# The same work in another order at three places: the opening, the end of the experts' stage, and the start of the second attention stage

## The chip, the core and the metric

The kernel runs on one core of a Trainium2 chip. The metric is the device time of one execution in microseconds; three runs of the kernel before gave 1770.38, 1770.89 and 1771.04, median 1770.89. Times in the trace count from the span's start.

## The reference

Six blocks with residual additions: an attention with 4 key heads, a cross attention over windows, a mixture of experts, then an attention with relative positions, a second cross attention and a second mixture of experts. The change touches the projections of the two self attentions (x is 2 batches of 1024 tokens of 256; 16 heads of 16) and the additions of the first experts' outputs:

```
# first self attention
q = (xn @ w_q).reshape(b, n, N_HEADS, D_HEAD).transpose(0, 2, 1, 3)
k = (xn @ w_k).reshape(b, n, KV_HEADS, D_HEAD).transpose(0, 2, 1, 3)
v = (xn @ w_v).reshape(b, n, KV_HEADS, D_HEAD).transpose(0, 2, 1, 3)
q = q * rf
k = k * rf
# first experts, last line
final = jnp.einsum('ebcm,bsec->bsm', expert_out, combine_mask)
# second self attention
qkv = (x @ W_qkv + b_qkv).reshape(b, s, 3, H, hd)
score = jnp.einsum('bhqd,bhkd->bhqk', q, k) + jnp.einsum('bhqd,qkd->bhqk', q, pe_k)
attn = jax.nn.softmax(score, axis=-1)
ctx = jnp.einsum('bhqk,bhkd->bhqd', attn, v) + jnp.einsum('bhqk,qkd->bhqd', attn, pe_v)
```

## The kernel before, in words

**Programs.** Each stage writes one program for each engine (PE, ACT, DVE, POOL, and SP, which issues the DMAs), and each engine works its program off in the order written. Engines meet at semaphores; between stages there is a barrier. So the order of the code is the order of the work, and an instruction that waits holds all that stands behind it on its engine.

**Splitting.** Queries and keys are needed to float32's precision in bf16 matmuls. Each tile of 128 x 512 (a unit) is split into three bf16 parts: high (a conversion), residue (tile minus high), middle (conversion of the residue), low (residue minus middle). The three parts go to DRAM with one store a unit, and are loaded back later in the layout that the matmuls want, 96 rows of six pairs of parts.

**Opening** (`Opening.run`). x is loaded in four groups, normalized, turned on PE (`turn`), and twelve units of q and k are made: `product` on PE, `rotate` on DVE (L396, L399), `high` on ACT (L319), `residue` on DVE (L408), the middle conversion on POOL (L353), `low` on DVE (L417), the store on SP (L237). There are four buffers of parts, and a unit may use one when the store of four units before has landed. From the fifth unit on, PE makes two tiles of values (L278) behind each product. From the seventh unit on, SP issues four loads of the first stage's queries and keys (L675, L679) behind a store, after all stores of the first half have landed.

**End of the experts' stage** (`experts`). While the last expert's outputs are stored and gathered again (POOL, 16 indirect DMAs for batch 1), batch 0's projections for the second attention are made, in eight pairs of a product and a value (`pair`), twelve units: `Heads.high` and `middle` on ACT (L565, L571), `residue`, `values` and `low` on DVE (L580, L593, L587), `store` on SP (L600), six buffers of parts. Between them DVE adds the gathered outputs of batch 1 to x (`add`, L2188, two a tile), sums up for the norm (`summed`, L2196 to L2201) and scales (`shifted`); ACT then normalizes (L2111) and PE turns (`turn`, L2050). The stage ends when every store has landed.

**Start of the second attention** (`attention1`). SP first issues the first group's twelve loads (four heads; L944 queries, L948 keys). Batch 1's projections follow in the same manner (five buffers), with three jobs called `relative` between them: PE multiplies the queries with the relative embeddings (L1169), ACT copies the result, POOL builds a band of it (`band_of`, L1272 and L1275; a band may be built when the one before has landed), SP writes the band to DRAM in a skewed layout (`band_out`, L1057) and reads it back into `dev` (`bands_in`, L1049), which POOL has set to zero before (L1301). Then 256 tiles follow: PE's scores (`row`, L1138), DVE's sum and maximum (L1341), ACT's exponentials, and so on. The first row waits for the last residue and value of the projections.

## Time and profile before

| | us |
|---|---|
| median of three runs | 1770.89 |
| profiled execution | 1768.36 |
| its span | 1766.6 |
| PE busy | 1562.5 (88%) |
| DVE busy | 1018.2 (58%) |
| ACT busy | 880.8 (50%) |
| POOL busy | 563.4 (32%) |

Shares over the whole span say little here, since the stages have different limits: PE bounds the experts and the tail, DVE the second attention. The three stretches of the change are short, and are read from the instructions in order of time, engine by engine, with what ended each idle time.

### The profile page before, as it was taken

To read this page: it belongs to the slowest core of one execution; us is meant where nothing else is said; L and a number is where in the kernel's file an instruction comes from. 1 tells how busy PE (TensorE), PEld (TensorE's weight loads), DVE (VectorE), ACT (ScalarE), POOL (GpSimd) and SP (SyncE) were. 2 spreads that over 40 slices of the span, in tenths; PEclk is the share of its full clock that TensorE was granted. 3 is DMA by queue.
4 is the path that set the end of the run, shared out by engine and by line. 5 is a ranking of instruction groups with operands and counts; after the bars stand their busy time and mean duration, and the time that the engine had idled before them with its cause. 6 is when DMAs were issued, how large, how long until landed. Compare 5 with 4: busy or idle time off the path is not lost. (4 is left out here: it accounts for less than half of the span.)

```text
span 1766.6 us, 34238 instructions
## 1 busy us (share of the span) xinstructions
PE 1562.5 (88%) x12792; PEld 1071.8 (61%) x12792; DVE 1018.2 (58%) x2084; ACT 880.8 (50%) x1468; POOL 563.4 (32%) x817
## 2 busy tenths in 40 slices
PE   7689989878479999999976799999999999996988
PEld 4233333256368767776753477777777777775544
DVE  6677777345332111111264788888888888873556
ACT  4156566632331111111134688888888888773421
POOL 3411111122313000000252455556555655542111
PEclk9799999997679999999987799999999999998999
DMA  5811111030123133221237796887868778645101
GB/s 153 237 26 29 24 24 24 2 132 22 39 75 131 63 119 128 87 86 60 61 112 153 208 222 195 203 205 200 205 200 202 210 197 200 185 137 174 49 12 36
DMA packets 209797, 213.06 MB, mean 121 GB/s; under 512 B 19652, under 2 KB 187218, under 8 KB 209506
## 3 DMA queue, kind: packets, MB, share of 16 engines
q1 hardware_dynamic: 204769, 197.24, 41.5%
q0 software_dynamic: 4864, 13.64, 2.3%
q8 instruction: 103, 1.69, 0.4%
q14 instruction: 61, 0.49, 0.1%
HBM read 128.82 MB, written 81.81 MB: 119 GB/s over the span
## 5 line engine op out<-in xcount | busy, mean ns | idle before, releaser
L1341 DVE CUSTOM_DVE_ANT_0 prob<-ps,dev 128x1024 f32<-128x1024 f32 x256 | 311.5, 1218 | 0.2 <-PE ps L1138 0.2
L1234 ACT ACTIVATE prob<-prob,nmax 128x1024 f32<-128x1024 f32 x256 | 293.3, 1146 | 8.3 <-DVE nmax L1341 8.3
L1158 PE MATMUL ps<-cst,prob 128*128 128x128 f32 x2048 | 279.4, 278 | 0.2
L2030 PE MATMUL ps<-xeT,w 128*128 128x384 f32 (+2 forms) x896 | 256.0, 447 | 5.1 <-DVE hT L2228 4.4
L1158 PEld LDWEIGHTS ps<-cst,prob 128*128 128x128 f32 x2048 | 228.3, 141 | 42.3 <-issue 21.0
L1370 DVE COPY probT<-ps 128x512 f32<-128x512 f32 x256 | 176.4, 689 | 104.1 <-PE ps L1158 104.0
L849 ACT ACTIVATE pT<-ps 128x512 f32<-128x512 f32 (+3 forms) x384 | 166.3, 495 | 119.3 <-PE ps L805 116.8
L887 DVE TENSOR_REDUCE nmax<-ps 128x1 f32<-128x128 f32 (+7 forms) x256 | 184.2, 753 | 69.1 <-PE ps L784 67.9
L2030 PEld LDWEIGHTS ps<-xeT,w 128*128 128x128 f32 x896 | 176.9, 198 | 77.6 <-DVE hT L2228 4.8
L2096 ACT ACTIVATE xT_c<-ps 128x256 f32<-128x256 f32 (+2 forms) x98 | 46.6, 476 | 326.0 <-PE ps L2030 325.9
L1244 ACT ACTIVATE probT<-ps 128x512 f32<-128x512 f32 x256 | 151.3, 591 | 102.4 <-PE ps L1158 102.2
L2228 DVE TENSOR_TENSOR hT<-ps,xT_c 128x256 f32<-128x256 f32 (+2 forms) x98 | 52.7, 538 | 223.4 <-ACT xT_c L2096 223.4
L1138 PE MATMUL ps<-ks,qs 96*128 96x512 bf16 (+4 forms) x768 | 155.7, 312 | 8.7 <-DVE vz L593 6.7
L1199 PE MATMUL ps<-probT,vg 128*18 128x128 f32 (+1 forms) x4096 | 135.9, 273 | 0.0
L2040 PE MATMUL ps<-vz,hT 128*128 128x256 f32 x560 | 124.2, 381 | 8.3 <-DVE hT L2228 8.3
L782 PE MATMUL ps<-ks,qs 96*128 96x512 bf16 (+3 forms) x384 | 107.5, 343 | 25.9 <-DVE nmax L887 17.7
L805 PE MATMUL ps<-qs,ks 99*128 99x512 bf16 (+3 forms) x384 | 110.0, 336 | 14.3 <-ACT pT L849 7.6
L875 POOL TENSOR_SCALAR_AFFINE_SELECT pT<-pT 128x512 f32<-128x512 f32 x64 | 40.6, 635 | 250.5 <-ACT pT L849 250.5
L2040 PEld LDWEIGHTS ps<-vz,hT 128*128 128x128 f32 x560 | 105.2, 190 | 24.9 <-DVE hT L2228 11.1
L2150 POOL DMA_DIRECT2D ybuf<-ye x32 | 20.4, 642 | 307.4 <-DVE ye L2251 307.4
L1199 PEld LDWEIGHTS ps<-probT,vg 128*18 128x18 f32 (+1 forms) x4096 | 106.4, 98 | 17.1 <-issue 16.6
L1281 POOL TENSOR_TENSOR wm<-pre,cst 128x256 f32<-128x256 f32 x128 | 93.9, 734 | 47.7 <-DMA pre<-skew_p 44.9
(317 smaller groups left out, 2167.4 us busy)
## 6 DMA issues: line engine op xcount, KB each, us to landing
dev<-skew_u SPq DMA_DIRECT2D x128, 256.0 KB, 3.6
skew_p<-prob SPq DMA_DIRECT2D x128, 256.0 KB, 3.3
w<-in_L_ffn_w SPq DMA_DIRECT2D x20, 896.0 KB, 6.3
skew_u<-cst SPq DMA_DIRECT2D x64, 256.0 KB, 4.0
pre<-skew_p SPq DMA_DIRECT2D x128, 128.0 KB, 2.9
qs<-qd SPq DMA_DIRECT2D x96, 128.0 KB, 3.8
ks<-kd SPq DMA_DIRECT2D x48, 256.0 KB, 5.8
vz<-in_L_ffn_w SPq DMA_DIRECT2D x10, 896.0 KB, 5.7
```

Of the source, the lines that this page charges most:

```text
L805: nc.tensor.matmul(ps[:, bank, 0:w], ks[:, j, kb * P:(kb + 1) * P], qs[:, j, r, q0:q0 + w], start=True, stop=True).then_inc(s_key, 1)
L849: nc.scalar.activation(pT[:, c % 2, r, 0:w], ps[:, ring_bank(job), 0:w], ACT.Exp).then_inc(s_exp, 1)
L887: nc.vector.tensor_reduce(nmax[:, n % 2, r * KB + a:r * KB + a + 1], slot[:, 0:w], AX.X, ALU.max, negate=True).then_inc(s_max, 1)
L1138: last = nc.tensor.matmul(ps[:, 2 * (t % 2) + lo // 512, lo % 512:lo % 512 + hi - lo], qs[:, n % 2, r, a * P:(a + 1) * P], ks[:, n % 2, r, ...
L1158: last = nc.tensor.transpose(ps[:, ring_bank(job), kb * P:(kb + 1) * P], prob_tile(t, (4 * h + kb) * P, (4 * h + kb + 1) * P), k.c("ident"))
L1199: last = nc.tensor.matmul(ps[r * VW:r * VW + wide, 7, q % 4 * P:q % 4 * P + P], vg[:, n % 2, r, kb, int(kb == a), 0:wide], probT[:, (HQ * ...
L1234: nc.scalar.activation(prob_tile(t, 0, S), prob_tile(t, 0, S), ACT.Exp, bias=nmax[:, t % 4:t % 4 + 1], scale=-1.0).then_inc(s_exp, 1)
L1244: nc.scalar.activation(probT[:, t % SLOTS, 0:512], ps[:, ring_bank(job), :], ACT.Copy).then_inc(s_evA, 1)
L1341: nc.vector.tensor_tensor_reduce(out=prob_tile(t, 0, S), in0=scores, in1=dev_tile(t), scale=-1.0, scalar=3.0e38, op0=ALU.add, op1=ALU.min, ...
L1370: nc.vector.tensor_copy(probT[:, t % SLOTS, 512:S], ps[:, ring_bank(job), :]).then_inc(s_evD, 1)
L2030: last = nc.tensor.matmul(ps[:, a + z * wide + h, 0:cols], w[:, j, c, f * P:(f + 1) * P], xeT[:, c, h * cols:(h + 1) * cols], start=(c == ...
L2040: last = nc.tensor.matmul(ps[0:w, a + t // 2, t % 2 * D:(t % 2 + 1) * D], hT[:, f, o:o + w], w2[:, j, f, :], start=(f == 0), stop=(f == FC ...
```

## The change

- **Opening:** the sixteen value products come behind all products; ACT makes the middle conversions, POOL the low subtractions; ACT's first two high conversions come ahead of two copies of turned tiles.
- **Order of units in `Heads`:** the first eight heads' queries and keys of both half sequences come first, so that the first six units complete the first heads.
- **Experts' end:** DVE's additions for batch 1 come ahead of most of the splitting; on PE, `turn(2)` comes behind the last pair; ACT's order follows. SP issues the first group's query loads (into memory that the experts' stage no longer uses) behind the ninth store, when the first six stores have landed, and the key loads behind the last store.
- **Second attention:** the head of SP's program has no loads; the first band goes out ahead of the first store, the second ahead of the second. PE begins with the first `relative`. DVE clears the first 3008 columns of `dev`, POOL the rest behind the first band.

```diff
         self.vz = self.sb("vz", [P, NH * KB * HD])
+        self.s_q0 = nc.alloc_semaphore(name="s_first_q")
+        self.s_k0 = nc.alloc_semaphore(name="s_first_k")
         self.qd1 = nc.dram_tensor("qd1", (3, NH, HD, S), BF16, kind="Internal").ap()
...
                         product(i)
-                        if i >= U - KB:
-                            value(2 * (i - U + KB))
-                            value(2 * (i - U + KB) + 1)
+                    for t in range(NT):
+                        value(t)
...
+                    def middle(i):
+                        rows = units[i][0]
+                        act.wait_ge(s_res, i + 1)
+                        nc.scalar.activation(parts[0:rows, i % NB, 1, :], res[0:rows, i % NB, :], ACT.Copy).then_inc(s_mid, 1)
                     def values(b):
...
                         normed(g)
+                    high(0)
+                    high(1)
                     turned(G - 2)
+                    middle(0)
                     turned(G - 1)
-                    for i in range(U):
-                        high(i)
-                        if i == U - 3:
-                            values(0)
+                    for i in range(2, U + 1):
+                        if i < U:
+                            high(i)
+                        middle(i - 1)
+                    values(0)
                     values(1)
...
                     last.then_inc(s_ws, 1)
+                    pool.wait_ge(s_id, 16)
+                    pool.wait_ge(self.s_cst, 16)
+                    nc.gpsimd.tensor_copy(cm[:, 0, :], k.c("causal"))
+                    nc.gpsimd.tensor_copy(cm[:, 1, :], k.c("ident"))
                     for i, (rows, *_) in enumerate(units):
...
                             pool.wait_ge(s_st[i % NB], 16 * (i // NB))
-                        nc.gpsimd.tensor_copy(parts[0:rows, i % NB, 1, :], res[0:rows, i % NB, :]).then_inc(s_mid, 1)
-                    pool.wait_ge(s_id, 16)
-                    pool.wait_ge(self.s_cst, 16)
-                    nc.gpsimd.tensor_copy(cm[:, 0, :], k.c("causal"))
-                    nc.gpsimd.tensor_copy(cm[:, 1, :], k.c("ident"))
+                        pool.wait_ge(s_mid, i + 1)
+                        nc.gpsimd.tensor_tensor(parts[0:rows, i % NB, 2, :], res[0:rows, i % NB, :], parts[0:rows, i % NB, 1, :],
+                                                ALU.subtract).then_inc(s_lo, 1)
...
                     summed(0)
...
                     shifted(G - 1)
-                    for i in range(U + 2):
+                    for i in range(U + 1):
                         if i < U:
                             rotate(i)
-                        if 0 < i <= U:
+                        if i:
                             residue(i - 1)
-                        if i > 1:
-                            low(i - 2)
...
+HQ1 = 4
+def first_group(k, ctx, tag):
+    return (k.sb("qs1first" + tag, [KS, HQ1, S], BF16, ctx=ctx), k.sb("ks1first" + tag, [KS, HQ1, 2, S], BF16, ctx=ctx))
+def load_part(sp, k, c, h, qs, ks, s_q, s_k):
+    if c < TERMS:
+        sp.dma_start(qs[c * HD:(c + 1) * HD, :, :], k.qd1[Q_PARTS[c], h:h + HQ1, :, :].rearrange("h d t -> d h t")).then_inc(s_q, 16)
+    else:
+        c -= TERMS
+        sp.dma_start(ks[c * HD:(c + 1) * HD, :, :, :].rearrange("d h z t -> d h (z t)"),
+                     k.kd1[K_PARTS[c], h:h + HQ1, :, :, :].rearrange("h d z t -> d h (z t)")).then_inc(s_k, 16)
 class Heads:
...
         self.prods, self.units = [], []
-        for q in (2 * b, 2 * b + 1):
-            for c in range(DC):
+        for c in range(DC):
+            for q in (2 * b, 2 * b + 1):
                 self.units.append((len(self.prods), q, k.qd1, b * H + HG * c, c))
                 self.prods.append((c * P, q))
-            for c in range(DC):
                 for z in range(2):
...
-    def stored(self, sp):
+    def stored(self, eng, upto=None):
+        upto = upto or len(self.units)
         for n in range(self.deep):
-            sp.wait_ge(self.s_st[n], 16 * ((len(self.units) - 1 - n) // self.deep + 1))
+            eng.wait_ge(self.s_st[n], 16 * ((upto - 1 - n) // self.deep + 1))
...
     with ExitStack() as ctx:
-        HQ = 4
-        qs = k.sb("qs1", [KS, 2, HQ, S], BF16, ctx=ctx)
-        ks = k.sb("ks1", [KS, 2, HQ, 2, S], BF16, ctx=ctx)
-        qd, kd = k.qd1, k.kd1
...
+        HQ = HQ1
+        first_group(k, ctx, "b")
+        q0, k0 = k.first
+        qs = (q0, k.sb("qs1", [KS, HQ, S], BF16, ctx=ctx))
+        ks = (k0, k.sb("ks1", [KS, HQ, 2, S], BF16, ctx=ctx))
...
-        front = ([("project", 0), ("project", 1), ("relative", 0), ("relative", 1)] + [("project", 2), ("relative", 2)] +
-                 [("project", n) for n in range(3, 9)])
+        front = ([("relative", 0), ("project", 0), ("relative", 1), ("project", 1), ("relative", 2)] +
+                 [("project", n) for n in range(2, 9)])
         order = front + list(steps())
...
-                for c in range(2 * TERMS):
-                    load(sp, 0, c, s_lq[0], s_lk[0])
-                for i in (0, 1):
-                    proj.store(sp, i)
                 band_out(0)
-                band_out(1)
+                proj.store(sp, 0)
                 bands_in(0)
                 bands_in(1)
-                for i in (2, 3):
+                band_out(1)
+                for i in range(1, 4):
                     proj.store(sp, i)
                 bands_in(2)
+                for i in range(4, 6):
+                    proj.store(sp, i)
                 band_out(2)
-                for i in range(4, len(proj.units)):
+                for i in range(6, len(proj.units)):
                     proj.store(sp, i)
...
                     r, a, n = t % HQ, t // HQ % KB, t // HQ // KB
-                    if r == 0 and a == 0:
-                        pe.wait_ge(s_lk[n % 2], LD * (n // 2 + 1))
+                    if r == 0 and a == 0 and n:
+                        pe.wait_ge(s_lk[n % 2], LD * ((n + 1) // 2))
+                    elif t == 0:
+                        pe.wait_ge(k.s_k0, LD)
                     if t >= 2:
...
                         a, n = q % KB, q // KB
-                        if a == 0:
-                            pe.wait_ge(s_lq[n % 2], LD * (n // 2 + 1))
+                        if a == 0 and n:
+                            pe.wait_ge(s_lq[n % 2], LD * ((n + 1) // 2))
+                        elif q == 0:
+                            pe.wait_ge(k.s_q0, LD)
...
-                nc.gpsimd.memset(dev[:, :], 0.0).then_inc(s_zero, 1)
                 band_of(0)
+                nc.gpsimd.memset(dev[:, THIRD:], 0.0).then_inc(s_zero, 1)
                 band_of(1)
...
             def _(dve):
+                nc.vector.memset(dev[:, 0:THIRD], 0.0).then_inc(s_zero, 1)
                 nc.vector.memset(prob[:, 0:SLOTS * PITCH].rearrange("p (s w) -> p s w", w=PITCH)[:, :, 0:PAD], 0.0)
...
     with ExitStack() as ctx:
+        with ExitStack() as over:
+            q0, k0 = k.first = first_group(k, over, "a")
+        hT = k.sb("hT", [P, FC0, ROWS], ctx=ctx)
+        xeT = k.sb("xeT", [P, DC, ROWS], ctx=ctx)
+        xe = k.sb("xe", [P, ST, D], ctx=ctx)
         wgt = k.sb("wgt", [P, B, 2, KB], ctx=ctx)
...
                     proj.store(sp, i)
+                    if i == 8:
+                        proj.stored(sp, 6)
+                        for c in range(TERMS):
+                            load_part(sp, k, c, 0, q0, k0, k.s_q0, k.s_k0)
+                for c in range(TERMS, 2 * TERMS):
+                    load_part(sp, k, c, 0, q0, k0, k.s_q0, k.s_k0)
                 proj.stored(sp)
...
                 def pair(n):
-                    pe.wait_ge(s_xt1, 2 if n < 4 else 4)
+                    pe.wait_ge(s_xt1, 2 if n < 2 else 4)
                     if n == 0:
...
                 turn(1)
-                for n in range(1, 6):
+                for n in range(1, KB):
                     pair(n)
                 turn(2)
-                pair(6)
-                pair(7)
                 turn(3)
...
                 act.wait_ge(s_bias1, 2)
-                for n in range(KB):
+                def highs(n):
                     for i in proj.of(n):
                         proj.high(act, i)
-                    if n == 0:
-                        turned(1)
-                    if n:
-                        for i in proj.of(n - 1):
-                            proj.middle(act, i)
-                    if n == 4:
-                        rooted(2)
-                        normed(2)
-                    if n == 5:
-                        turned(2)
-                for i in proj.of(KB - 1):
-                    proj.middle(act, i)
+                def middles(n):
+                    for i in proj.of(n):
+                        proj.middle(act, i)
+                highs(0)
+                turned(1)
+                for n in range(1, 4):
+                    highs(n)
+                    middles(n - 1)
+                rooted(2)
+                highs(4)
+                middles(3)
+                normed(2)
+                for n in range(5, KB):
+                    highs(n)
+                    middles(n - 1)
+                turned(2)
                 rooted(3)
                 normed(3)
+                middles(KB - 1)
                 turned(3)
...
                 shifted(1)
-                for n in range(KB):
+                def residues(n):
                     for i in proj.of(n):
...
                     proj.values(dve, n)
-                    if n:
-                        for i in proj.of(n - 1):
-                            proj.low(dve, i)
-                    if n == 4:
-                        shifted(2)
+                def lows(n):
+                    for i in proj.of(n):
+                        proj.low(dve, i)
+                residues(0)
+                add(KB)
+                for n in (1, 2):
+                    residues(n)
                     add(KB + n)
-                    if n == 3:
-                        summed(2)
+                    lows(n - 1)
+                add(KB + 3)
+                summed(2)
+                residues(3)
+                lows(2)
+                add(KB + 4)
+                shifted(2)
+                residues(4)
+                lows(3)
+                add(KB + 5)
+                residues(5)
+                add(KB + 6)
+                lows(4)
+                residues(6)
+                add(KB + 7)
                 summed(3)
-                for i in proj.of(KB - 1):
-                    proj.low(dve, i)
+                lows(5)
+                residues(7)
                 shifted(3)
+                lows(6)
+                lows(7)
...
 def tail_order():```

SP's queue around the border between the experts' stage and the second attention; `qd` and `kd` are the stores of parts, `qs` and `ks` the loads, `skew_u` a band out, `dev` bands in. Before:

```order
L600 DMA kd<-parts 128x3x512 x4
L1942 UNCONDITIONAL_BRANCH
L1039 UNCONDITIONAL_BRANCH
L944 DMA qs<-qd 16x4x1024 x6
L948 DMA ks<-kd 16x4x2048 x6
L600 DMA qd<-parts 128x3x512 x2
L1057 DMA skew_u<-cst 128x4x128 x2
L1049 DMA dev<-skew_u 128x2x256 x2
L600 DMA kd<-parts 128x3x512 x2
```

The same place of the kernel changed:

```order
L618 DMA kd<-parts 128x3x512 x2
L517 DMA qs1firsta<-qd 16x4x1024 x6
L618 DMA qd<-parts 128x3x512
L618 DMA kd<-parts 128x3x512 x2
L520 DMA ks1firsta<-kd 16x4x2048 x6
L1955 UNCONDITIONAL_BRANCH
L1049 UNCONDITIONAL_BRANCH
L1067 DMA skew_u<-cst 128x4x128
L618 DMA qd<-parts 128x3x512
L1059 DMA dev<-skew_u 128x2x256 x2
L1067 DMA skew_u<-cst 128x4x128
L618 DMA kd<-parts 128x3x512 x2
```

The loads moved from behind the barrier (the two branches) to ahead of it, the queries ahead of three stores too, and the bands moved ahead of stores.

DVE's last work in the experts' stage; `x<-xn_c` is an addition, `stats1a` begins a summing, `parts<-res,parts` is a low part, `res` a residue. Before:

```order
L580 SCALAR_TENSOR_TENSOR res<-ps,pre,parts 128x512 x2
L593 TENSOR_TENSOR vz<-ps,pre 128x16x16
L587 TENSOR_TENSOR parts<-res,parts 128x512 x2
L2188 SCALAR_TENSOR_TENSOR x<-xn_c,wgt,x 128x256 x2
L2196 BN_STATS stats1a<-x 128x6 x4
L2199 BN_AGGR mean_var<-stats1a 128x2 x4
L2201 TENSOR_SCALAR rstd<-mean_var 128x4
L587 TENSOR_TENSOR parts<-res,parts 128x512 x2
L2206 RECIPROCAL rstd<-rstd 128x4
L2207 SCALAR_TENSOR_TENSOR shift1a<-mean_var,rstd 128x4
```

The same place of the kernel changed:

```order
L2213 SCALAR_TENSOR_TENSOR x<-xn_c,wgt,x 128x256 x2
L2221 BN_STATS stats1a<-x 128x6 x4
L2224 BN_AGGR mean_var<-stats1a 128x2 x4
L2226 TENSOR_SCALAR rstd<-mean_var 128x4
L605 TENSOR_TENSOR parts<-res,parts 128x512 x2
L598 SCALAR_TENSOR_TENSOR res<-ps,pre,parts 128x512 x2
L611 TENSOR_TENSOR vz<-ps,pre 128x16x16
L2231 RECIPROCAL rstd<-rstd 128x4
L2232 SCALAR_TENSOR_TENSOR shift1a<-mean_var,rstd 128x4
L605 TENSOR_TENSOR parts<-res,parts 128x512 x3
```

The last summing moved ahead of two residues, a value and three low parts.

## Rows read from the trace of the kernel before

**Rows 1.** The page's head, and DVE's long group of the second attention

```profile
span 1766.6 us, 34238 instructions
...
L1341 DVE CUSTOM_DVE_ANT_0 prob<-ps,dev 128x1024 f32<-128x1024 f32 x256 | 311.5, 1218 | 0.2 <-PE ps L1138 0.2
```

**Rows 2.** PE in order of time, opening: start, us, what, [idle before <-releaser]

```profile
23.47 3.60 PE L270 MATMUL ps<-xT,wqkv 128*128 128x512 f32 x8
...
45.93 1.10 PE L278 MATMUL ps<-wqkv,xT 128*128 128x64 f32 x8
54.15 0.26 PE L782 MATMUL ps<-ks,qs 96*128 96x128 bf16 x1 [7.11 <-PEq L202]
```

**Rows 3.** SP's seventh and last store, opening, and how long stores took to land

```profile
39.83 0.37 SPq L237 DMA_DIRECT2D qd<-parts  x1
...
50.81 0.59 SPq L237 DMA_DIRECT2D kd<-parts  x1
...
DMA to landing us min/median/max: 2.5/3.1/4.0
```

**Rows 4.** SP in order of time, 935 to 976

```profile
939.70 5.21 SPq L600 DMA_DIRECT2D kd<-parts  x4
949.68 2.68 SPq L944 DMA_DIRECT2D qs<-qd  x6
952.40 2.77 SPq L948 DMA_DIRECT2D ks<-kd  x6
959.68 4.70 SPq L600 DMA_DIRECT2D qd<-parts  x2
964.42 11.83 SPq L1057 DMA_DIRECT2D skew_u<-cst  x2
```

**Rows 5.** The six query loads, then the six key loads: issue ns, starts, landing

```profile
L944 SPq DMA_DIRECT2D qs<-qd x6: 333/422/426, 949.7 to 951.9; - x6
...
DMA to landing us min/median/max: 2.9/4.3/5.6
...
L948 SPq DMA_DIRECT2D ks<-kd x6: 426/426/427, 952.4 to 954.7; - x6
...
DMA to landing us min/median/max: 7.3/11.6/15.5
```

**Rows 6.** All 24 stores of L600: from issue to landing

```profile
DMA to landing us min/median/max: 2.5/3.6/11.3
```

**Rows 7.** ACT in order of time, start of the second attention

```profile
971.06 0.69 ACT L565 ACTIVATE parts<-ps,pre 128x512 bf16<-128x512 f32 x1 [7.18 <-DMA qd<-parts]
...
982.37 0.69 ACT L565 ACTIVATE parts<-ps,pre 128x512 bf16<-128x512 f32 x1 [7.97 <-DMA kd<-parts]
```

**Rows 8.** The same stretch: DVE's first maximum, POOL's clearing, PE's first product

```profile
994.82 1.21 DVE L1341 CUSTOM_DVE_ANT_0 prob<-ps,dev 128x1024 f32<-128x1024 f32 x1
...
949.68 6.24 POOL L1301 MEMSET dev<- 128x7360 f32 x1 [20.54 <-POOLq L139]
...
949.72 3.75 PE L543 MATMUL ps<-xT,pre 128*128 128x512 f32 x4 [2.06 <-PEq L139]
```

**Rows 9.** POOL's conversions in the opening, and its additions of two tiles later

```profile
L353 POOL CAST parts<-res x12: 1004/1012/1400, 25.7 to 49.0; 128x512 bf16<-128x512 f32 x8, 64x512 bf16<-64x512 f32 x4
...
L1275 POOL TENSOR_TENSOR cst<-cst x32: 1261/1282/1287, 960.6 to 1550.2; 128x508 f32<-128x508 f32 x32
```

**Rows 10.** DVE in order of time, end of the experts' stage

```profile
930.05 0.75 DVE L580 SCALAR_TENSOR_TENSOR res<-ps,pre,parts 128x512 f32<-128x512 f32 x1 [1.73 <-ACT parts L565]
...
941.29 1.41 DVE L2196 BATCH_NORM_STATS2 stats1a<-x 128x6 f32<-128x256 f32 x4
...
943.23 1.29 DVE L587 TENSOR_TENSOR parts<-res,parts 128x512 bf16<-128x512 f32 x2
```

**Rows 11.** ACT's last normalizing and its last copy in the experts' stage

```profile
944.84 2.08 ACT L2111 ACTIVATE xn_c<-x,shift1a,rstd 128x256 f32<-128x256 f32 x4 [1.28 <-DVE shift1a L2207]
...
947.69 0.60 ACT L2117 ACTIVATE xT<-ps 128x512 f32<-128x512 f32 x1 [0.30 <-PE ps L2050]
```

35 lines of the change are left out of this document (7 added, 28 removed).

## The prediction

> **What bounds the kernel now.** I read the page first: one core, a span of 1766.6 us, and the row of the long second attention stage, where DVE's maxima stand almost without idle time [rows 1]. That stage is bound by DVE from its first maximum on, so whatever starts it earlier shortens the kernel by as much, and nothing inside it is changed. The change touches three stretches, and I read each in the order of time of its engines: the opening (to 54 us), the end of the experts' stage (905 to 950) and the start of the second attention stage (950 to 995).
>
> In the opening the reader is to see that PE sets the pace at its end: two products take 3.60 us, 1.77 to 1.80 each, but the last product ends only at 45.93, because two values stand behind each, and the next stage's first matmul comes at 54.15 [rows 2]. Between lie the last unit's steps on four engines and its store, issued at 50.81 [rows 3].
>
> At the border at 950 the reader is to see a queue of transfers. SP issues six query and six key loads of the first group there, then two stores, then a band [rows 4]. The query loads end 0.97 us apart, the sixth at 951.9 + 5.6 = 957.5; the key loads end about 2.1 apart, the sixth at 954.7 + 15.5 = 970.2 [rows 5]. Everything issued later lands after that: the store of 959.68 has the longest landing of its line, 11.3, so 971.0 [rows 6]. ACT, which needs the buffer, stands 7.18 us until 971.06, then 7.97 until 982.37 [rows 7]. The second wait has another link: SP held its next stores behind the second band, issued at 964.42 + 11.83 - 0.36 = 975.9, because POOL may build that band only when the first has landed. The first maximum comes at 994.82 [rows 8], 24.6 after the last key.
>
> **Opening, part by part.** Removed from PE's product chain: the values between. Nine products from 23.47 at 1.77 end at 39.5, 6.4 before 45.93. The sixteen values behind them take at most 8 x 1.10 = 8.8 [rows 2], to 48.3, and ACT's two copies 1.2: hidden as long as the last store lands later than about 49.5; if it doesn't, they are the end. Moved: the middle conversion from POOL to ACT, the last subtraction from DVE to POOL. ACT has the room: it now makes two conversions of about 0.6 a unit. POOL's conversions took 1.01 each; its additions of two tiles, 508 columns, took 1.28 [rows 9]. The subtraction has no row of its own; its bounds are 1.01 and twice that, and I take 1.28, the nearest row. What is late next is SP: behind the seventh store (39.83) it issues four loads before the next, which the old pace hid. The seventh product ends at 23.47 + 4 x 1.77 = 30.6; the steps behind it (four of about 0.65, the kinds of rows 7 and 10, the subtraction, and 0.4 of hand-offs: 4.3) and 1.3 of waiting for one of four buffers make 36.2. SP then waits for the sixth store (to 37.4), issues four loads (2.0) and the eighth store at 39.5, landed 3.1 later [rows 3] at 42.6. The last unit needs that buffer: four steps, 3.9 with hand-offs, and its store goes out at 46.5 instead of 50.81. It lands 2.8 to 3.9 later, behind loads and stores issued shortly before it, at 49.3 to 50.4; before, it landed some 0.5 ahead of the 54.15 of rows 2, at 53.6. Gain 3.2 to 4.3; I take 3.5. With POOL at 2.02 a unit it is 0.6: twelve of them from 24.4 end at 48.6 at the earliest, some 50 with the waits for buffers, and the landing makes 53. The attention stage behind starts all its queues at the barrier, so its start moves whole.
>
> For this price there is a rule that speaks against the change. The Trainium skill, "GPSIMD Engine Reference", section "Engine selection", says that elementwise work with two inputs is about twice as slow on GpSimd as on VectorE and that one input runs near line rate. By it the sum would be that of the first rival below; rows 9 show 1.28 against 1.01 for two inputs against one, so the trace agrees with a surcharge and not with its size.
>
> **End of the experts' stage.** DVE's work is the same; its order changes. The ninth to sixteenth additions go ahead of the splitting, PE's third turn goes behind the last pair, so that the wait of 1.73 at 930.05 goes [rows 10], and some 3.6 us of residues and low parts go behind the last summing. The summing, which ended at 943.2, ends at about 937.5. Then two low parts (1.2), the last residues and value (1.6), the shift (0.35): 940.6. ACT normalizes (2.08 [rows 11]) to 942.7; queued behind that on ACT are now the last two middle conversions (1.1), and DVE's last low parts wait for them: 944.6. (ACT's root of the third group also stands further ahead now, before the fifth pair's high parts, and PE's pairs queue behind; but what it waits for is a sum of DVE's, which is busy throughout.) Before, the low parts ended at 943.23 + 1.29 = 944.5 [rows 10]. So ACT is done 3.6 sooner than 947.69 + 0.60, but the last store still goes out at 944.9 [rows 4]; I count 0, between -1 and +1.
>
> Added on SP: six query loads behind the ninth store (about 939.1) and ahead of the last three, six key loads behind all. The query loads drain in 7.8 (949.7 to 957.5 [rows 4, 5]), to 946.9. The three stores land behind them at about 1.15 each, 950.4, where the last one landed at 944.5 + 3.6 = 948.1 [rows 6]. The stage's end waits for stores, not for key loads: the next stage begins 2.3 later, at 952.0. That is the price of the loads; its bounds are 0 (they slip in beside the stores) and 3.3.
>
> **Start of the second attention stage.** Here I walk the queues of all engines forward with the durations of the rows. Removed: 5.5 us of issuing at its head, and the queue. The key loads, issued by 948, drain in 12.9 behind the stores: 963.3, 6.9 before 970.2. Moved ahead: the first band needs only the query loads; it is issued at about 955.6 (952.0 and 0.4 for a first matmul, 0.7 for ACT's copy, 2.4 for POOL's two steps), because POOL no longer clears 7360 columns first (6.24 [rows 8]). DVE clears 3008 of them, 2.6 at POOL's rate, beside PE's first product of 3.75, so for nothing; with a product at full clock it would cost up to 1. From the last key the chain is: first band lands 0.8 later (964.1); POOL builds the second (2.4 and hand-offs: 966.7); SP issues it and at once the second store (967.5), landed 3.8 later, 971.3; ACT goes on, and high, residue, middle, low bring the fifth store at 973.8, landed 976.9; the seventh goes out at 976.8 and lands 3.05 later, 979.9, which frees the last unit; high, two residues, value, 2.6: first row 982.5, 2 us of matmul, first maximum 984.5. The same walk over the kernel before ends at 993.7 where the trace has 994.8, so I add 1.1: 985.6, a gain of 9.2. Bounds: 6.9 (all of the 24.6 behind the last key stays) and 12.3 (nothing delayed at the border and the keys no longer the gate, by the same walk: 982.5).
>
> **Sum.** 3.5 + 9.2 = 12.7 from the profiled execution's 1768.36 (span 1766.6 and 1.8 around it) is 1755.7. That execution lies 2.5 under the median of the runs, 1770.89, so I forecast 1758.2 for the median.
>
> **Rivals.**
> 1. POOL's subtraction costs twice its conversion (2.02). Then the opening gives 0.6 and the sum is 9.8: 1761.1. For it: no row has the new operation with these types. Against: the 32 additions of rows 9, of nearly its size, lie at 1.26 to 1.29.
> 2. The waits change place. Five buffers, and SP in order: the second to fourth stores now stand behind the second band, the fifth behind the third load of bands. If the seventh high waits as long as the row of 7.97 [rows 7] instead of the 3.7 of my walk, 4.3 go back: 1762.5. For it: this very link made that wait. Against: its cause, a band landing after 8.8 behind the keys, starts 9 us earlier.
> 3. The border costs nothing: gain 12.3 + 3.5: 1755.1. For it: from 939.70 to 949.68 the queue carried the last four stores alone [rows 4]. Against: queues drained in order in rows 5 and 6.
> 4. Slower: the query loads hold the border. They stand on SP ahead of the last three stores, for which the barrier waits, and the keys come behind. Every us of their drain beyond 7.8 delays all that follows by one, so the gain is gone at 20.5 (3.4 a load). If the six drained one after the other, each at the 4.3 median of its own landing [rows 5], it would be 25.8, 18 more: 1776.2. Against: rows 5 have them 0.97 apart.
>
> **How the numbers follow.** Forecast 0.66, rival 1 0.08, rival 2 0.14, rival 3 0.08, rival 4 0.04. All but the last are faster. From 1754.4 (12.3 + 4.2) to 1763.4 (6.9 + 0.6) go the bounds of the sum; with rival 2 and some mixing of the cases I give 1754.0 to 1764.5. What a measurement of this kernel can tell from no change is 0.2%, 3.5 us: faster 0.92, within 0.03 + 0.02 (rival 4 at half its price, or several small losses) 0.05, slower 0.03.
>
> **What would show it.** Right: the second stage's first matmul near 50.6; POOL's subtraction at 1.2 to 1.4; the seventh to tenth stores of the opening spaced by SP's loads; the border behind the experts 2 us later against the work ahead of it, with ACT long done; ACT's longest wait in the front below 4.5; the first maximum 45.1 - 33.6 = 11.5 sooner after the border than now. Wrong: a border that moves by more than 4; a sixth key landing more than 14 behind the border; a POOL subtraction of 2 us; any wait of DVE's maxima that wasn't there.

## The result, and the profile after

The changed kernel takes 1759.87 us (median of 4 runs, 1758.57 to 1760.65), the kernel before 1770.64 in the same comparison: ratio 0.9939, 95% interval 0.9922 to 0.9956, so 7.8 to 13.8 us less. The forecast was 1758.2, a gain of 12.7 on the profiled execution; the medians differ by 10.8. Three executions of the comparisons below, 1798.98 and 2602.84 of the kernel before and 7876.53 of experiment 3, lie far above all others and are left out of the medians here, so that experiment 3 stands at 1755.19 and not at the 1755.4 that the texts on record name. The two profiled executions differ by only 7.7 (1768.36 and 1760.65), and that needs a word first, since all terms are read from such executions.

The page's head and DVE's long group (answer to [rows 1]):

```profile
span 1758.9 us, 34234 instructions
...
L1354 DVE CUSTOM_DVE_ANT_0 prob<-ps,dev 128x1024 f32<-128x1024 f32 x256 | 311.6, 1218 | 2.4 <-DMA skew_p<-prob 2.3
```

The maxima take what they took, 311.6, but wait 2.4 instead of 0.2. PE in the opening, in order of time, of the changed kernel (answer to [rows 2]):

```profile
15.28 7.63 PE L272 MATMUL ps<-xT,wqkv 128*128 128x512 f32 x12 [0.36 <-ACT xT L312]
...
24.64 16.44 PE L272 MATMUL ps<-xT,wqkv 128*128 128x512 f32 x36
41.01 7.36 PE L280 MATMUL ps<-wqkv,xT 128*128 128x64 f32 x64
52.50 0.26 PE L801 MATMUL ps<-ks,qs 96*128 96x128 bf16 x1 [4.13 <-PEq L204]
```

The first twelve matmuls took 7.63; in the profile of before the same twelve took 6.33. That is not the change: the changed kernel profiled a second time (experiment 11 below) has

```profile
15.46 6.34 PE L272 MATMUL ps<-xT,wqkv 128*128 128x512 f32 x12 [0.36 <-ACT xT L312]
...
23.54 16.44 PE L272 MATMUL ps<-xT,wqkv 128*128 128x512 f32 x36
39.91 7.36 PE L280 MATMUL ps<-wqkv,xT 128*128 128x64 f32 x64
51.36 0.26 PE L801 MATMUL ps<-ks,qs 96*128 96x128 bf16 x1 [4.09 <-PEq L204]
```

and no wait of 2.4 (0.2 there). In PE's weight loads one sees what differs: beside the slow matmuls a load takes 0.34 us, beside the others 0.19, and in the first profile the step from one to the other comes between 18.82 and 19.59, in that of before between 16.39 and 17.14 (columns as above):

```profile
18.82 0.34 PEld L272 LDWEIGHTS ps<-xT,wqkv 128*128 128x128 f32 x1 [0.52 <-issue]
19.59 0.19 PEld L272 LDWEIGHTS ps<-xT,wqkv 128*128 128x128 f32 x1 [0.43 <-issue]
```

```profile
16.39 0.34 PEld L270 LDWEIGHTS ps<-xT,wqkv 128*128 128x128 f32 x1 [0.52 <-issue]
17.14 0.19 PEld L270 LDWEIGHTS ps<-xT,wqkv 128*128 128x128 f32 x1 [0.41 <-issue]
```

So PE works its first products at half its pace for a stretch whose length differs between executions. The granted clock, the column behind POOL's, seems to speak against a lower clock, since it reads 1.00 (2.4 GHz) here in the first profile:

```profile
15.00:20.00 5.00, 4.72 (x6) 2.04 (x7) 1.60 (x9) 3.92 (x11) 0.00 (x0) 1.00 0.03 3
```

But the column takes off only what a record of a lower clock covers, and the trace's first record of the clock, one of 1.00, begins at 19.50 in this profile, at 17.02 in that of before and at 17.10 in the changed kernel's second. In all fourteen traces it begins between the last weight load of 0.34 and the first of 0.19, or within the latter. So the 1.00 says nothing on what came before; half the pace there is what the lower level (1.2 GHz) would give, without a record that shows it. (The Trainium skill, "TensorE: Matmul & The Clock Gate", Part 1, says that the number of matmuls at the lower clock at a kernel's start varies from run to run; here the trace agrees on a start that varies.) Pairs of executions must therefore start alike. Of before (first products 6.33, span 1766.6) and the changed kernel's second profile (6.34, span 1756.3) the difference is 10.3, which fits the medians.

The border, SP in order of time (answer to [rows 4]; the x is the number of issues):

```profile
937.07 0.96 SPq L618 DMA_DIRECT2D kd<-parts  x2
938.27 3.33 SPq L517 DMA_DIRECT2D qs1firsta<-qd  x6
941.64 0.43 SPq L618 DMA_DIRECT2D qd<-parts  x1
942.96 0.96 SPq L618 DMA_DIRECT2D kd<-parts  x2
943.96 3.39 SPq L520 DMA_DIRECT2D ks1firsta<-kd  x6
956.33 0.38 SPq L1067 DMA_DIRECT2D skew_u<-cst  x1
964.06 0.38 SPq L618 DMA_DIRECT2D qd<-parts  x1
964.54 1.09 SPq L1059 DMA_DIRECT2D dev<-skew_u  x2
965.69 0.53 SPq L1067 DMA_DIRECT2D skew_u<-cst  x1
966.27 1.10 SPq L618 DMA_DIRECT2D kd<-parts  x2
```

From issue to landing, the last two stores and then the six key loads (answer to [rows 5, 6]):

```profile
L618 SPq DMA_DIRECT2D kd<-parts x2: 360/368/377, 943.0 to 943.6; - x2
...
DMA to landing us min/median/max: 7.1/7.2/7.4
```

```profile
L520 SPq DMA_DIRECT2D ks1firsta<-kd x6: 427/448/714, 944.0 to 946.9; - x6
...
DMA to landing us min/median/max: 7.6/9.5/11.9
```

The last store lands at 943.6 + 7.4 = 951.0, and the second attention begins at 952.61; before, it began at 949.72 [rows 8] with the work ahead of it 0.78 later (PE's first pair at 905.75 against 904.97). So the border cost 2.89 + 0.78 = 3.7. PE's first pair in the profile of before; then first pair and first matmul of the second attention in the changed kernel's first profile and in its second:

```profile
905.75 1.98 PE L543 MATMUL ps<-xT,pre 128*128 128x512 f32 x4 [0.74 <-ACT xT L2117]
```

```profile
904.97 1.98 PE L561 MATMUL ps<-xT,pre 128*128 128x512 f32 x4 [0.74 <-ACT xT L2134]
...
952.61 0.58 PE L1182 MATMUL ps<-relk,qs1firsta 96*128 96x128 bf16 x4 [10.18 <-PEq L141]
```

```profile
902.55 1.98 PE L561 MATMUL ps<-xT,pre 128*128 128x512 f32 x4 [0.74 <-ACT xT L2134]
...
952.21 0.58 PE L1182 MATMUL ps<-relk,qs1firsta 96*128 96x128 bf16 x4 [10.80 <-PEq L141]
```

Counted the same way, the border cost 5.7 in the second profile (49.66 from pair to matmul, against 43.97 before): 1.4 more ahead of DVE's last summing, where PE's seventh product took 3.62 instead of 2.68 at a granted clock of 0.55 instead of 0.66 (924 to 929), and 0.6 more behind it. The sixth key lands at 946.9 + 11.9 = 958.8 in the first profile, not at the forecast 963.3. The waits and the first maximum, on ACT, POOL and DVE (answer to [rows 7, 8]):

```profile
972.03 0.69 ACT L583 ACTIVATE parts<-ps,pre 128x512 bf16<-128x512 f32 x1 [3.79 <-DMA kd<-parts]
...
977.74 0.69 ACT L583 ACTIVATE parts<-ps,pre 128x512 bf16<-128x512 f32 x1 [1.93 <-DMA kd<-parts]
```

```profile
956.24 3.73 POOL L1314 MEMSET dev<- 128x4352 f32 x1
959.93 1.05 POOL L1284 TENSOR_TENSOR cst<-cst,pre 128x512 f32<-128x512 f32 x1
```

```profile
953.27 2.56 DVE L1340 MEMSET dev<- 128x3008 f32 x1 [9.74 <-PEq L141]
...
986.07 1.21 DVE L1354 CUSTOM_DVE_ANT_0 prob<-ps,dev 128x1024 f32<-128x1024 f32 x1
```

From PE's first matmul behind the border to the first maximum: 33.46 (32.78 in the second profile), forecast 33.6, before 45.10.

### The profile page after: what moved, and what is told of

It reads as the page before. It is cut to its first block and busy times, and to the rows that moved or that the text cites. A ratio compares the mean times of both kernels' runs of the same rounds, so it can differ in the third digit from the quotient of the medians.

```text
span 1758.9 us, 34234 instructions
## 1 busy us (share of the span) xinstructions
PE 1562.0 (89%) x12792; PEld 1069.8 (61%) x12792; DVE 1013.5 (58%) x2073; ACT 886.9 (50%) x1480; POOL 562.2 (32%) x817
## 5 line engine op out<-in xcount | busy, mean ns | idle before, releaser
L1354 DVE CUSTOM_DVE_ANT_0 prob<-ps,dev 128x1024 f32<-128x1024 f32 x256 | 311.6, 1218 | 2.4 <-DMA skew_p<-prob 2.3
L801 PE MATMUL ps<-ks,qs 96*128 96x512 bf16 (+3 forms) x384 | 107.2, 342 | 22.6 <-DVE nmax L906 17.3
L1299 POOL TENSOR_TENSOR cst<-wm 128x64 f32<-128x64 f32 x128 | 41.0, 320 | 181.7 <-DVE pre L1386 175.3
```

The costliest lines, as they stand in the source:

```text
L801: last = nc.tensor.matmul(ps[:, bank, 0:hi - lo], query, ks[0:KS, j, lo:hi], start=True, stop=hi < w)
L1354: nc.vector.tensor_tensor_reduce(out=prob_tile(t, 0, S), in0=scores, in1=dev_tile(t), scale=-1.0, scalar=3.0e38, op0=ALU.add, op1=ALU.min, ...
```

## The experiments

All with five rounds, each against the kernel before on the same chip. There were three chips, and the medians of before differ by 1.4 between them, so kernels of different chips are compared by their ratios here (0.0010 is 1.8 us). "Stage 2" is PE's first matmul behind the opening; "border" runs from DVE's last summing (its first statistics) to its clearing at the head of the second attention; "front" from there to the first maximum. These are read from the profiled execution, whose first twelve matmuls stand beside them. Where DVE's summing or clearing stands elsewhere than in the changed kernel, a cell is empty or counts from PE's first matmul. "Kernel 3" is that of experiment 3.

| kernel | median | ratio to before, 95% | first 12 | stage 2 | border | front |
|---|---|---|---|---|---|---|
| before | 1769.66 to 1771.04 | 1 | 6.33 | 54.15 | | 45.1 from PE's first matmul |
| changed | 1759.87 | 0.9939 (0.9922 to 0.9956) | 7.63 | 52.50 | 18.86 | 32.80 |
| changed, again | 1758.10 | 0.9932 (0.9918 to 0.9947) | 6.34 | 51.36 | 19.47 | 32.12 |
| 1 opening alone | 1765.71 | 0.9975 (0.9964 to 0.9986) | 7.72 | 52.70 | | 43.6 from PE's |
| 2 all but the opening | 1763.93 | 0.9958 (0.9943 to 0.9974) | 7.91 | 55.69 | 19.58 | 32.94 |
| 3 queries behind 7th store | 1755.19 | 0.9919 (0.9906 to 0.9932) | 6.44 | 51.79 | 16.66 | 31.29 |
| 4 loads at the head | 1764.34 | 0.9969 (0.9958 to 0.9980) | 7.44 | 52.14 | 14.99 | 43.11 |
| 5 = 3, low part on DVE | 1756.95 | 0.9927 (0.9909 to 0.9944) | 7.83 | 52.03 | 16.57 | 33.13 |
| 6 = 3, keys behind band | 1759.85 | 0.9945 (0.9927 to 0.9962) | 6.73 | 51.81 | 15.16 | 38.16 |
| 7 = 3, additions between | 1757.33 | 0.9931 (0.9914 to 0.9948) | 6.35 | 51.30 | | 32.84 |
| 8 = 3, old front | 1762.70 | 0.9962 (0.9950 to 0.9974) | 7.46 | 52.32 | 16.13 to PE's | 37.42 from PE's |
| 9 = 3, three keys early | 1761.09 | 0.9943 (0.9929 to 0.9957) | 6.59 | 51.54 | 21.15 | 31.66 |
| 10 = 9, stores ahead of band | 1758.89 | 0.9931 (0.9916 to 0.9946) | 6.62 | 51.70 | 20.94 | 31.20 |
| 12 = 3 and 10's move | 1756.46 | 0.9918 (0.9904 to 0.9931) | 7.40 | 52.54 | 16.75 | 32.16 |

**1 and 2: the two halves apart.** The first is before with the changed opening (the engines' blocks of the opening and nothing else), the second the changed kernel with the opening of before.

> The kernel before with the opening of the changed kernel and nothing else of it. Theory: the opening's gain is real but smaller than the 3.5 that was forecast, and what is lacking has two parts: 1.2 us in which PE ran its first products at half pace (12 matmuls in 7.63 instead of 6.33; a matter of the execution, not of the change), and some 0.7 from DVE's residues, which stretch to 1.04 to 1.65 us beside POOL's new subtractions instead of 0.67. Then the next stage's first matmul comes 1.7 earlier where the first products take 7.6, 2.9 earlier where they take 6.3, and the median is 1767.8 to 1769.0. Rival 1: the opening's gain doesn't reach the end, 1770.6. Rival 2: the 3.5 were right and the profiled execution of the changed kernel was an exception, 1767.1.

> The changed kernel with the opening of the kernel before. Theory: the two parts of the change add up; without the opening's 1.7 to 2.9 the median is 1761.6 to 1762.8, and the stretch from the border at 950 to the first maximum reads as in the changed kernel (33.5 us). Rival: the opening is worth nothing by the end, 1759.9.

Measured, by medians: 4.3 less for the opening alone (by the interval 2.5 to 6.4), 6.1 less for the rest (4.6 to 10.1); the sum, 10.4, is the whole change's 10.8 within the error. Both medians lie outside what the theory gave, the first 2 below, the second 1 above, so by the medians it had put the opening too low. The stretches show why: executions that start alike give 54.15 to 51.36 (2.8) where the first products are quick, and 55.69 to 52.50 or 52.70 (3.2 or 3.0) where they are slow. That before's opening has slow first products too (7.91 in the second) clears the change of them. The first rival, a gain that doesn't reach the end, falls.

**3 and 4: where the loads stand.** The third moves the six query loads two stores ahead:

```
-                    if i == 8:
+                    if i == 6:
                         proj.stored(sp, 6)
```

> The changed kernel with the six query loads of the first group behind the seventh store of the experts' stage instead of the ninth. Theory: the border came 3.7 later against the work ahead of it because the query loads stood ahead of the last three stores, which landed 6.0 to 7.4 us after their issue. Between the seventh store at 932.4 and the eighth at 937.1 the queue is empty, so the query loads can drain there: the last stores land 3 to 4 after their issue, the second attention begins 3 to 3.7 earlier against the experts' summing, and the median is 1756 to 1757. Rival: the last stores are held by the key loads behind them or by the pace of landing as such, and it stays at 1759.9. A third way: the loads now hold the eighth and ninth stores, DVE and ACT wait for the buffers, and it is slower, 1761 or more.

The fourth puts all twelve where they were, at the head of the second attention:

```
+                for c in range(2 * TERMS):
+                    load_part(sp, k, c, 0, q0, k0, k.s_q0, k.s_k0)
                 band_out(0)
                 proj.store(sp, 0)
...
-                    if i == 8:
...
-                        for c in range(TERMS):
-                            load_part(sp, k, c, 0, q0, k0, k.s_q0, k.s_k0)
-                for c in range(TERMS, 2 * TERMS):
-                    load_part(sp, k, c, 0, q0, k0, k.s_q0, k.s_k0)
```

> The changed kernel with all twelve loads of the first group at the head of the second attention, as in the kernel before; the order of bands, stores and products, the split clearing and everything else stay as changed. Theory: the early loads are worth most of the gain at the border. The border comes 3.7 sooner, but the first matmul waits 7.8 for the sixth query load, and the first band lands behind the keys at 21 us behind the border instead of 7; the first maximum comes 41 to 47 us behind the border instead of 33.5, and the median is 1764 to 1770. Rival: the gain comes from the bands that go ahead of the stores and from the split clearing, and the loads only change places; then it stays between 1757 and 1760.

The third has the lowest median of the study, 1755.19, with experiment 12 beside it; by the ratios it is 3.5 under the changed kernel and 2.3 under its second measurement, with intervals that overlap. SP's row and the landing of the last store:

```profile
931.65 2.80 SPq L517 DMA_DIRECT2D qs1firsta<-qd  x6
935.68 0.98 SPq L618 DMA_DIRECT2D kd<-parts  x2
```

```profile
L618 SPq DMA_DIRECT2D kd<-parts x1: 360/360/360, 942.2 to 942.2; - x1
DMA to landing us min/median/max: 5.2/5.2/5.2
```

It lands 5.2 after its issue instead of 7.4 (8.0 in the second profile), and the border is 2.2 shorter (2.8), where the theory had 3 to 3.7: the keys behind the last store still slow it, as its rival said (experiment 6). The front is 1.5 shorter (0.8). In the fourth PE stands idle for 14.35 until the queries land, the last 7.4 of it after DVE has begun its clearing, and the first maximum comes 43.1 behind the clearing, 10.3 later, for a border 3.9 shorter:

```profile
956.52 0.61 PE L1184 MATMUL ps<-relk,qs1firsta 96*128 96x128 bf16 x4 [14.35 <-DMA qs1firsta<-qd]
```

So 6.4 net by the stretches, and 5.3 or 6.5 by the ratios (against the changed kernel's first and second measurement), is what the early loads are worth; the theory had 41 to 47 and 1764 to 1770, and both came. (This execution is the longest of the kernel's seven, so only its stretches are read.)

**5: what POOL's subtraction does to DVE.** POOL's loop goes, and DVE gets the low part back:

```
-                    for i in range(U + 1):
+                    for i in range(U + 2):
...
+                        if i > 1:
+                            low(i - 2)
```

> The kernel with the query loads behind the seventh store (median 1755.4), with the opening's last subtraction back on DVE; the middle conversion stays on ACT, the values stay last, and POOL has nothing to do there. Theory: the opening gave 2.4 to 3.0 and not 3.5 because two of DVE's residues stretch to 1.64 us beside POOL's subtractions, and because POOL's subtraction takes 1.36 and stands behind it. On DVE alone a unit takes 3 x 0.6 = 1.8, which is the pace of PE's products, and every residue and subtraction reads 0.67 to 0.69. The last store then goes out near 45.5, the values end near 47.3 where the products start at 23.5, and the next stage's first matmul comes at 49.6 to 50.5 (51.8 before): 1753.3 to 1754.3. Rival: SP's twelve loads and the landings set the end, and it stays at 51.5 or more and at 1755.4. If the residues stretch without POOL's subtractions too, POOL is not what stretches them.

In the changed kernel, DVE's residues and POOL's subtractions in the opening read (min/median/max ns):

```profile
L420 DVE TENSOR_TENSOR res<-f,parts x12: 670/684/1646, 22.1 to 45.5; 128x512 f32<-128x512 f32 x8, 64x512 f32<-64x512 f32 x4
```

```profile
L368 POOL TENSOR_TENSOR parts<-res,parts x12: 1142/1274/1599, 25.3 to 47.2; 128x512 bf16<-128x512 f32 x8, 64x512 bf16<-64x512 f32 x4
```

and the residues of this experiment:

```profile
L413 DVE TENSOR_TENSOR res<-f,parts x12: 673/676/691, 22.0 to 45.1; 128x512 f32<-128x512 f32 x8, 64x512 f32<-64x512 f32 x4
```

POOL's subtractions are what stretched them: that part is shown. It is worth little: stage 2 begins at 52.03, with products from 24.82, against 52.50 with products from 24.64, so 0.65 sooner, and the time doesn't show it (by the ratios 1.4 slower than kernel 3, with intervals that overlap). The rest of the opening hangs on SP, as the rival said:

```profile
37.74 0.37 SPq L239 DMA_DIRECT2D qd<-parts  x1
...
40.89 0.42 SPq L239 DMA_DIRECT2D qd<-parts  x1
...
47.84 0.67 SPq L239 DMA_DIRECT2D kd<-parts  x1
```

The eighth store leaves 3.2 behind the seventh, behind four loads that wait for the sixth store's landing; ACT then waits 2.95 for that buffer, and the last store lands 3.6 after its issue.

**6: are the keys what the front waits for?** In kernel 3, the six key loads go from behind the last store to behind the first band:

```
                 band_out(0)
+                for c in range(TERMS, 2 * TERMS):
+                    load_part(sp, k, c, 0, q0, k0, k.s_q0, k.s_k0)
                 proj.store(sp, 0)
...
-                for c in range(TERMS, 2 * TERMS):
-                    load_part(sp, k, c, 0, q0, k0, k.s_q0, k.s_k0)
```

> The kernel with the query loads behind the seventh store, with the six key loads behind the first band in the second attention instead of behind the last store of the experts' stage. Theory: the landing order decides. The last store no longer shares the queue with the keys (landing 3 us after its issue instead of 5.2), so the border comes 1.9 sooner, and the first band lands 3.4 after its issue instead of behind the last key (6.8). But the first stores now land behind the keys, at some 16 behind the border instead of 13.4, and ACT waits for their buffers: the two cancel, median 1754.5 to 1756.5, with the wait before ACT's sixth conversion longer by 2 to 3. Rival: the first band is what the front waits for, and the whole 2 to 5 come off: 1750.5 to 1753.5.

The border is 1.5 shorter and the last store lands 3.7 after its issue instead of 5.2, so the keys behind it do slow it. But the front is 6.9 longer and the time by the ratios 4.6 higher:

```profile
967.48 0.69 ACT L583 ACTIVATE parts<-ps,pre 128x512 bf16<-128x512 f32 x1 [6.22 <-DMA qd<-parts]
```

In kernel 3 this wait is 0.51. The mechanism of the theory, stores that land behind the keys, was right, its price too small; the rival, that the first band alone matters, is out.

**7: the order of DVE's additions.** Kernel 3 with each of the ninth to sixteenth additions behind its pair, as before the change:

```
-                def residues(n):
+                for n in range(KB):
                     for i in proj.of(n):
                         proj.residue(dve, i)
                     proj.values(dve, n)
...
+                    if n:
+                        for i in proj.of(n - 1):
+                            proj.low(dve, i)
...
                     add(KB + n)
```

> The kernel with the query loads behind the seventh store, with DVE's order at the experts' end as before the change: each of the ninth to sixteenth additions behind the residues and low parts of its pair (ACT's last two middle conversions go ahead of its last root, since DVE's low parts now stand ahead of the last shift). Theory, as in the prediction: this part is worth nothing (-1 to +1), since the last store goes out when DVE's low parts are done, and DVE's work is the same; 1754.5 to 1756.5, ACT's last copy 3 to 4 later and still ahead of the last store's landing. Rival: ACT's normalizing, now 3.6 later, ends behind the last store's landing and holds the border: 1757 to 1759.

1757.33 against 1755.19, by the ratios 2.1 slower, with intervals that overlap by more than half; by the trace the second attention begins at 948.26 (949.03 in kernel 3, whose PE was 0.3 later at 902) and the first maximum comes at 981.76 (980.98). ACT's last copy now ends at 945.3, still ahead of the landing. The zero of the prediction holds to within some 2 us (PE's third turn stays where the change put it, so its place was not tried).

**8: the order of the front.** Kernel 3 with the front of before:

```
-        front = ([("relative", 0), ("project", 0), ("relative", 1), ("project", 1), ("relative", 2)] +
+        front = ([("project", 0), ("project", 1), ("relative", 0), ("relative", 1)] + [("project", 2), ("relative", 2)] +
...
+                for i in (0, 1):
+                    proj.store(sp, i)
                 band_out(0)
-                proj.store(sp, 0)
+                band_out(1)
...
+                nc.gpsimd.memset(dev[:, :], 0.0).then_inc(s_zero, 1)
                 band_of(0)
```

> The kernel with the query loads behind the seventh store, with the start of the second attention in the order of before: projections ahead of the relative products, two stores ahead of the bands, and POOL clearing all of 7360 columns first; the early loads stay. Theory: loads and order each hold the same chain, so undoing either gives back most: the first band goes out behind the second store, 15 behind the border instead of 3.7, the second band at 21.5 and the stores behind it at 22.5 instead of 14, and the first maximum comes 38 to 41 behind the border instead of 31.3: 1762 to 1765. Rival: with the keys early the order of bands and stores doesn't matter, 1755 to 1757.

By the ratios 7.6 slower than kernel 3, and the first maximum 37.4 behind PE's first matmul instead of 31.95. The wait of before is back, with its cause, the second band that holds SP for 7 us:

```profile
963.43 7.01 SPq L1067 DMA_DIRECT2D skew_u<-cst  x2
```

```profile
977.16 1.42 ACT L583 ACTIVATE parts<-ps,pre 128x512 bf16<-128x512 f32 x2 [9.41 <-DMA kd<-parts]
```

Of the four combinations, then, from PE's first matmul (in the fourth experiment from SP's first load, 948.45): neither 45.1, order alone 43.8, loads alone 37.4, both 32.0. The order is worth 1.3 without the loads and 5.5 with them. DVE's share of the clearing went with the order; the two were not tried apart.

**9, 10, 12: a better place for keys and stores.** 9 puts three key loads into the gap behind the ninth store; 10 also sends the second and third store ahead of the second band; 12 is that last move on kernel 3.

```
+                    if i == 8:
+                        for c in range(TERMS, TERMS + 3):
+                            load_part(sp, k, c, 0, q0, k0, k.s_q0, k.s_k0)
-                for c in range(TERMS, 2 * TERMS):
+                for c in range(TERMS + 3, 2 * TERMS):
```

```
                 bands_in(1)
+                for i in range(1, 3):
+                    proj.store(sp, i)
                 band_out(1)
```

> The kernel with the query loads behind the seventh store, with three of the six key loads behind the ninth store and three behind the last. Theory: of the 3.9 us that the loads cost the changed kernel at the border, 2.2 come from the query loads ahead of the last three stores and 1.5 from the key loads behind the last store, which slow its landing; and the first band lands 1 us behind the last key. With three keys in the gap behind the ninth store, the last key lands 3 to 5 sooner, the first band lands at 3.4 instead of 6.8 behind its issue, the second band and the next stores go out 1 to 1.5 sooner, and the last store lands within 1 of where it did: first maximum 30 to 31 behind the border (31.9 before), 1753 to 1755. Rival: the three keys hold stores ten to twelve as the query loads did in the changed kernel, the border comes 1 to 3 later, and it is 1755.5 to 1758.

> The same with the second and third store of the second attention ahead of the second band. Theory: what is left in the front is ACT's wait of 3.5 for the landing of the second store, which stands behind the second band (256 KB, some 1 us of landing); ahead of it, the wait is 1 shorter and the first maximum 0.5 to 1 sooner, 1752 to 1755. Rival: the third band, for which POOL then waits longer, holds SP's later stores, as the second band did in the kernel before, and the wait goes to ACT's ninth conversion: no gain or up to 2 slower.

> The two moves that helped, together: the query loads behind the seventh store of the experts' stage (all key loads behind the last store, as in the changed kernel), and in the second attention the second and third store ahead of the second band. Theory: they act at different places and add: the border as with the query loads behind the seventh store (16.6 from the last summing to DVE's clearing), ACT's wait before its seventh conversion 1.5 to 2 instead of 3.5, and the first maximum 30.8 to 31.2 behind DVE's clearing (31.3 without the second move); 1754 to 1755.5. Rival: with the border early the first band, behind the keys, sets when the second goes out, and the stores ahead of it push POOL's third band and so the later stores: 1755.5 to 1757.

Nine: the rival, and dearer than it said. The last two stores land 9.3 and 9.7 after their issue, and the border is 4.5 longer than in kernel 3:

```profile
L618 SPq DMA_DIRECT2D kd<-parts x2: 360/368/377, 941.0 to 941.6; - x2
DMA to landing us min/median/max: 9.3/9.5/9.7
```

Ten does in the trace what it should: ACT's wait goes from 3.49 to 1.60, the first maximum comes 0.46 sooner behind the clearing, but the wait behind it grows to 2.12, so the rival takes most of it; the medians can't tell 9 from 10 apart with certainty. Twelve, 1756.46, is no better than kernel 3: the wait of 3.48 becomes 2.14, and before the tenth conversion one of 1.13 becomes 2.38. Its rival had the time and a wait that changes place right.

**11: the changed kernel once more**, for its profile above.

> The changed kernel once more, beside the two others. Theory: the 1.2 us by which PE's first twelve matmuls took longer in its profile are the execution's, not the change's, and about as much again follows by 905; an execution whose first products take 6.3 to 6.7 begins the next stage at 51.3 to 51.8 and lies 2 us below one where they take 7.4 to 7.9. The border stays 3.5 to 4 late, the median is 1758.5 to 1761. Rival: the profile was as the kernel always is, or the median of four runs was off by over 1.5.

Stage 2 began at 51.36, the span is 2.6 shorter, and the wait of 2.4 on DVE was the first execution's alone. The border stayed long, 19.47 from the summing and by the count from PE's first pair 5.7 late, where 3.5 to 4 were expected; the median, 1758.10, is 0.4 under the expected range.

## Why the prediction was right

It forecast 1758.2 with a range of 1754.0 to 1764.5; the changed kernel took 1759.87 and, measured again, 1758.10. That it came so near is in part luck. The sum gave 1755.7 for a profiled execution, and the two took 1760.65 and 1758.07; the 2.5 added for the median, read from one profile of before, did not come back (the changed kernel's profiles lie 0.8 above its median and at it). In the two executions that start alike (before, and the changed kernel's second profile) the gain is 10.3 instead of 12.7: 2.8 up to stage 2, 0.4 from there to PE's first pair, 6.6 from the pair to the first maximum (5.7 lost at the border, 12.3 won in the front; forecast 9.2 in all) and 0.4 behind. Step by step:

- **Opening, 3.5 forecast, 2.8 to 3.2 measured** in executions that start alike. The chain was the one forecast (values out of the way, four loads ahead of the eighth store, a late last store). Its sizes were off: in the second profile the last store left at 47.36 with products from 23.54 (46.5 forecast), since POOL held DVE's residues (in experiment 5, without POOL's part, it left 0.8 sooner behind the products' start); it then needed 3.4 to land. POOL's subtraction took 1.27 at the median, where 1.28 was taken, so the first rival (2.02) falls; but that it fits so well is luck, since it took 1.15 undisturbed and up to 1.60 where a residue of DVE's was under way (last section). The rule of the Trainium skill was not wrong there but misread in the prediction: "GPSIMD Engine Reference", "Engine selection", puts two-input work on GpSimd at about twice VectorE's time, and 1.15 undisturbed or 1.27 at the median against DVE's 0.68 for the same subtraction (experiment 5) is 1.7 or 1.9 times. The prediction had doubled POOL's own conversion instead.
- **Experts' end: zero for the order, right** (experiment 7). **Border 2.3 forecast, bound 3.3, measured 3.7 and in the second profile 5.7: this step failed,** and by the second the prediction's own sign of being wrong (a border that moves by more than 4) is met. It said that the stage's end waits for stores and not for key loads. The stores were slowed from both sides: by the query loads ahead of them (18.86 against 16.66 in kernel 3: 2.2) and by the keys issued after them (16.66 against 15.16 in experiment 6: 1.5), with 15.0 where no load stands there (experiment 4). The first is the 2.3 of the prediction. The second it excluded, because landings came in the order of issue in [rows 5, 6]. They still did, as far as the semaphores tell: in all fourteen traces what SP issued from 900 to 1000 landed in that order. But to land first is not to land undisturbed: the last store lands 5.2 after its issue with the keys behind it, 3.7 without (experiments 3 and 6). (The Trainium skill, "DMA: Bandwidth & Descriptors", "Queues, rings and completion order", says that completion is not first in, first out per issuing engine; no run here shows that.)
- **Front, 33.6 forecast, 33.46 and 32.78 measured: right in its sum, by other links, and so in part by luck.** In the first profile the keys drained 1.5 apart instead of 2.1 and were done at 958.8, 4.5 ahead of the forecast; the first band landed at 956.33 + 3.4 = 959.7, 0.9 behind them (0.8 forecast), when POOL had just cleared. But the gain went: PE's first product and value took 3.72 and 1.85 at a granted clock of 0.50 (1.2 GHz; 953 to 958), the first store, which waits for DVE's low part, left at 964.06 (11.45 behind PE's first matmul; 10.40 in kernel 3, where that value took 1.03 at a granted clock of 1.00), and SP in order let the second band out only at 965.69 and the second store at 966.27, 1.2 ahead of the forecast. From there the walk held: ACT's wait 3.79 (3.7 forecast), DVE's clearing 2.56 (2.6), hidden.
- **Rival 2**, waits that change place, happened in small (1.93 and 0.96 behind the 3.79) and cost nothing net. **Rival 3** falls with experiment 4. **Rival 4**, the slower one, did not come: the queries landed 4.3 to 5.3 after their issue.
- **After the first maximum** 1.05 of the 8.75 went in the first profile, with the wait of 2.3 for a landing that the kernel's second profile has not. That is the execution's.

Not settled: why the opening alone came out at 4.3 by its medians and at some 3 by its trace, though the interval (2.5 to 6.4) holds both; what stretched the border from 3.7 to 5.7 beyond the slower product; and what of the opening's gain belongs to the values and what to the middle conversions, since only the subtraction was moved by itself.

## What to carry to other kernels

A transfer put ahead of time into a queue that drains before a barrier is paid twice, by the stores behind it and by those just ahead of it; look for a gap in the issuing engine's row (here 4.3 us behind the seventh store: with the query loads there the border was 2.2 shorter), and count what fits: three key loads in the gap behind the ninth store made it 4.5 longer. Two changes that shorten the same chain from both ends are worth less apart than together (1.3 and 7.7, together 13.1), so test them together. Before two profiled executions are compared, see whether they start alike, and read each stretch by itself.

## What was not expected of the hardware

- DVE's subtraction with two inputs in SBUF took up to 1.64 instead of 0.67 beside POOL's; without POOL's it is 0.67 to 0.69. POOL's took 1.15 undisturbed and up to 1.60 where a residue of DVE's had begun just ahead of it. From the changed kernel's opening, POOL's rows first, in order of time:

```profile
25.28 1.16 POOL L368 TENSOR_TENSOR parts<-res,parts 128x512 bf16<-128x512 f32 x1 [11.38 <-ACT parts L325]
27.27 2.71 POOL L368 TENSOR_TENSOR parts<-res,parts 128x512 bf16<-128x512 f32 x2 [0.83 <-ACT parts L325]
```

```profile
27.17 0.68 DVE L420 TENSOR_TENSOR res<-f,parts 64x512 f32<-64x512 f32 x1
...
28.89 1.65 DVE L420 TENSOR_TENSOR res<-f,parts 128x512 f32<-128x512 f32 x1
```

  Of POOL's pair the first took 1.60 and the second 1.15. The residue of 28.89 ends 0.6 behind POOL's second subtraction, about its own length: as if it had begun only then. POOL's first, issued while the residue of 27.17 ran, ends 1.0 behind that one: again nearly its own length. (The Trainium skill, "SBUF — State Buffer", "Who interferes with whom", has it so: a DVE instruction with two SBUF inputs and a GpSimd instruction that reads SBUF exclude each other, and the later one waits.) In the front of kernel 3 two low parts took 2.52 instead of 1.28 in the same way.
- PE's first twelve matmuls took between 6.33 and 7.91, in kernels with either opening, according to how long the half pace lasted, and the difference is not made good: from stage 2 to PE's first pair of the experts' end it takes 850.9 to 851.6 in the seven executions with quick first products (6.33 to 6.73) and 852.2 to 853.3 in the seven with slow ones (7.40 to 7.91).
